# A four-layer graph network on one core: the degree sums of the first layer are added up across a block's four quarters on VectorE

## Chip, core and metric

One Trainium2 chip, one of its cores. The metric is the device time of one execution in microseconds (us); the time before is the median of three runs.

## What is computed

Four graph layers over 4096 nodes with 128 features, each on a layer-normalised, rectified copy of `x`, with a residual. Only the first layer is touched here:

```python
h = jnp.maximum(_layernorm(x, axis=-1), 0.0)
inv_deg = 1.0 / (jnp.sum(adj, axis=1) + beta)
agg = adj @ h + beta[:, None] * h
x = x + inv_deg[:, None] * agg @ kernel + bias
```

`adj` is 4096 x 4096 in float32 and mostly zero. The later layers use its nonzero entries alone, so the first layer's pass over `adj` also finds them and writes lists of them.

## The kernel before

The matrix passes through on-chip memory once, transposed by the host, in `NB` = 8 blocks of 512 destination nodes. A block is 8 MB and comes in four quarters (slots) of 2 MB; slot `q` is `ring[:, q, :, :]`, 128 partitions x 8 tiles x 512 nodes. Blocks 0 and 1 are written out, blocks 2 to 7 are one hardware loop. Each engine has its own program, and they meet at semaphores.

In block `nb`, with `last` = `nb - 1` and `before` = `nb - 2` (the lists run one to two blocks behind the loads):

- **TensorE** (`block0` of `pe`): per slot 8 products of 128x512 that add into `ps[:, 0, :]` (L1719); after the last slot four more for the `beta` term (L1726). Between the slots it makes the lists of the block before: `a_list` (L1698, 32 small products), `fold` (L1705), `places` (L1688, L1689). Then it waits for all four slots' sums, makes the degrees as products with a column of ones (L1745), waits for `agg_out` and makes `agg @ kernel` (L1753). `places` for the next block waits for `flag_ready`, which is the last thing that VectorE does in a block.
- **VectorE** (`block0` of `dve`): per slot `reduce_slot`, which adds the slot's 8 tiles down to one row of 512 sums a partition in three steps: 2048 elements (L1216), 1024 (L1217), 512 (L1221), the last into `degp[:, q, :]`. Between them the lists: `place` (L1108 to L1131), `code` (L1140, L1142, L1145; its last step releases `a_list`), `list_quarters` (L1151, waits for `a_list`), `lists` (L1163 to L1166, releases the gathers), `update` (L1232 to L1240, needs the degrees), the copy of `ps[:, 0, :]` to `aggT` (L1269, `agg_out`) and `mark` (L1100, `flag_ready`).
- **ScalarE** (`see`): for a block 128 passes over 128x128 pieces that find which hold nonzeros (L888), and the loads of the next block's slots (`load_quarter`), each when TensorE, VectorE and ScalarE have all read the slot.
- **GpSimd** gathers the listed rows of `adj` (L705, with their indices copied at L696), as the lists become ready.

A `Link` orders dependent VectorE instructions: each one counts up a semaphore, and VectorE waits for that count and passes a `nop` (`settle`) before the next one:

```python
def __call__(self, ins):
    self.n += 1
    ins.then_inc(self.s, 1)
    self.dve.wait_ge(self.s, self.base + self.n)
    settle(self.dve)
```

Of the kernel before, what the change touches and what calls it, by code (L numbers as in the profile page):

```python
# [24 lines left out]
ALU = mybir.AluOpType  # L25
# [3 lines left out]
P = 128  # L29
# [7 lines left out]
NQ = 4  # L37
# [35 lines left out]
def build(nc, x, adj_rows, k0, b0, beta, hv, w2, b2, wq, bq, wkvs, bkvs, wb, out, h1_table, h2_table, kv_table,  # L73
          adj_table, mask_table):
    ctx = ExitStack()
    with ctx:
        def sb(name, shape, dt=F32):
            return ctx.enter_context(nc.sbuf_tensor(name, shape, dt))

        def sem(name):  # L80
            return ctx.enter_context(nc.semaphore(name))
# [10 lines left out]
        ones = sb("ones", [P, P])  # L92
# [77 lines left out]
        degp = work[:, 20480:22528].rearrange("p (q n) -> p q n", q=NQ)  # L170
        half_sum = work[:, 16384:18432].rearrange("p (m n) -> p m n", m=MQ // 2)
        quarter_sum = work[:, 18432:19456].rearrange("p (m n) -> p m n", m=MQ // 4)
# [43 lines left out]
        ps = ctx.enter_context(nc.psum_tensor("ps", [P, 8, 512], F32))  # L216
# [84 lines left out]
        link_sum = sem("link_sum")  # L301
        slot_full = [sem(f"slot_full{q}") for q in range(NQ)]
        slot_used = [sem(f"slot_used{q}") for q in range(NQ)]
        slot_summed = [sem(f"slot_summed{q}") for q in range(NQ)]
# [4 lines left out]
        deg_done = sem("deg_done")  # L309
# [25 lines left out]
        def settle(eng):  # L335

            eng.nop(nofuse=True)
# [695 lines left out]
        def _(dve):  # L1033
# [178 lines left out]
            def reduce_slot(nb, q):  # L1212

                dve.wait_ge(slot_full[q], 16 * nb + 16 if not isinstance(nb, int) else 16 * (nb + 1))
                link = Link(dve, link_sum, 2, nb * NQ + q)
                link(nc.vector.tensor_tensor(half_sum, ring[:, q, 0:MQ // 2, :], ring[:, q, MQ // 2:MQ, :], ALU.add))  # L1216
                link(nc.vector.tensor_tensor(quarter_sum, half_sum[:, 0:MQ // 4, :], half_sum[:, MQ // 4:MQ // 2, :], ALU.add))  # L1217
                link.end()
                if q == 0:
                    dve.wait_ge(deg_done, nb + 1)  # L1220
                nc.vector.tensor_tensor(degp[:, q, :], quarter_sum[:, 0, :], quarter_sum[:, 1, :],  # L1221
                                        ALU.add).then_inc(slot_summed[q], 1)

# [21 lines left out]
            def block0(nb, last, before):  # L1245

                reduce_slot(nb, 0)
                if last is not None:
                    place(last)
                if before is not None:  # L1250
                    list_quarters(before, 3)
                    lists(before, 2)
                if last is not None:
                    code(last, 0)
                    update(last)
                if before is not None:
                    lists(before, 3)
                reduce_slot(nb, 1)
                if last is not None:
                    code(last, 1)  # L1260
                    list_quarters(last, 0)
                reduce_slot(nb, 2)
                if last is not None:
                    lists(last, 0)
                    code(last, 2)
                    list_quarters(last, 1)
                reduce_slot(nb, 3)
                dve.wait_ge(agg_done, nb + 1)
                nc.vector.tensor_copy(aggT[:, :], ps[:, 0, :]).then_inc(agg_out, 1)  # L1269
                if last is not None:  # L1270
                    lists(last, 1)
                    code(last, 3)
                    list_quarters(last, 2)
                mark(nb)
# [17 lines left out]
            link = Link(dve, link_s, 2)  # L1292
# [20 lines left out]
            link = Link(dve, link_s, 2, 1)  # L1313
# [131 lines left out]
            link = Link(dve, link_w, 1)  # L1445
# [3 lines left out]
            for n, rows in enumerate((wkvs_sb, bkvs_bc)):  # L1449
                ins = nc.vector.tensor_tensor_reduce(out=junks[:, n, :], in0=rows[:, 2 * P:3 * P], in1=wb_bc[:, P:2 * P], scale=1.0,  # L1450
                                                     scalar=0.0, op0=ALU.mult, op1=ALU.add,
                                                     accum_out=rows[:, 3 * P:3 * P + 1])
# [29 lines left out]
            def row_stats2(tiles):  # L1482
                for t in tiles:
                    ins = nc.vector.bn_stats(stats[:, t, :], x_sb[:, t, :])
                return ins
# [12 lines left out]
            for n in (2, 3):  # L1498
                rest2(n + 1, slice(FT * n, FT * n + FT))
                for m in range(4):  # L1500
                    t = 4 * n - 6 + m
                    products(t, t % TB)
                    ins = row_stats2(range(FT * n + 2 * m, FT * n + 2 * m + 2))
# [144 lines left out]
        def _(pe):  # L1648
            mm = nc.tensor.matmul
# [33 lines left out]
            def places(nb):  # L1683

                pe.wait_ge(flag_ready, nb + 3)
                pe.wait_ge(place_read, nb + 1)
                flags = flag[:, :, :].rearrange("p t m -> p (t m)")
                mm(ps[:, 5, 128:256], tri[:, :], flags, start=True, stop=True)  # L1688
                mm(ps[:, 5, 256:384], ones_b[:, :], flags, start=True, stop=True).then_inc(place_done, 1)  # L1689

            def a_list(nb, j):

                n = nb * TB + j
                pe.wait_ge(coded_ready, n + 1)
                pe.wait_ge(list_read, n + 1)
                for m in range(T):
                    g = m % 4
                    ins = mm(ps[NC * g:NC * g + NC, 7 if j % 2 else 3, 0:P], coded[:, j % 2, 0, :, m], onehot[:, j % 2, :, m],  # L1698
                             start=(m < 4), stop=(m >= T - 4))
                ins.then_inc(list_done, 1)  # L1700

            def fold(nb, j):

                pe.wait_ge(list_out, nb * TB + j + 1)
                mm(ps[:, 7 if j % 2 else 3, P:P + NC], quarters[:, j % 2, :], sel[:, :], start=True, stop=True).then_inc(fold_done, 1)  # L1705

            def block0(nb, last, before):
                pe.wait_ge(agg_out, 1 + nb)
                if last is not None and before is not None:
                    places(last)  # L1710
                for q in range(NQ):
                    pe.wait_ge(slot_full[q], 16 * (nb + 1))
                    for m in range(MQ):
                        t = q * MQ + m
                        if last is None and t < T // 2:
                            pe.wait_ge(ht_ready[0], t + 1)
                        elif last is None:
                            pe.wait_ge(half_relu, (t - T // 2) // TB + 1)
                        ins = mm(ps[:, 0, :], h_sb[:, q * MQ + m, :], ring[:, q, m, :],  # L1719
                                 start=(q + m == 0), stop=False)  # L1720
                    if q < NQ - 1:
                        ins.then_inc(slot_used[q], 1)
                    else:
                        pe.wait_ge(hbeta_ready, nb + 1)
                        for j in range(TB):
                            ins = mm(ps[:, 0, j * P:(j + 1) * P], hbeta[:, j, :], ident[:, :], start=False, stop=(j == TB - 1))  # L1726
                        ins.then_inc(agg_done, 1)
                    if q == 0 and last is not None and before is None:
                        places(last)
                    if q == 0 and before is not None:  # L1730
                        fold(before, 2)
                        a_list(before, 3)
                    if q == 1 and before is not None:
                        fold(before, 3)
                    if q and last is not None:
                        if q == 3:
                            fold(last, 1)
                        a_list(last, q - 1)
                        if q == 2:
                            fold(last, 0)  # L1740
                for q in range(NQ):
                    pe.wait_ge(slot_summed[q], nb + 1)
                for j in range(TB):
                    for q in range(NQ):
                        ins = mm(ps[:, 6, j:j + 1], degp[:, q, j * P:(j + 1) * P], ones[:, 0:1],  # L1745
                                 start=(q == 0), stop=(q == NQ - 1))
                ins.then_inc(deg_done, 1)
                if last is None:
                    pe.wait_ge(ld, 16 * NLD)
                pe.wait_ge(up_used, 1 + nb)  # L1750
                pe.wait_ge(agg_out, nb + 2)
                for j in range(TB):
                    ins = mm(ps[:, 1, j * P:(j + 1) * P], aggT[:, j * P:(j + 1) * P], k0_sb[:, :], start=True, stop=True)  # L1753
                ins.then_inc(up_done, 1)

            block0(0, None, None)
            block0(1, 0, None)
            with pe.Fori(2, NB) as nb:
                block0(nb, nb - 1, nb - 2)
# [191 lines left out]
```

## Time and profile before

| | |
|---|---|
| median of three runs | 1194.56 us (1192.62 to 1199.07) |
| the profiled execution | 1195.47 us, its span 1193.8 us |
| TensorE matmul busy | 895.6 us of the span (75%) |
| VectorE busy | 835.5 us (70%) |
| ScalarE busy | 681.3 us (57%) |
| GpSimd busy | 656.0 us (55%) |
| first layer with its lists | about the first 440 us of the span |

The shares are means over layers with different limits, so what the change is worth has to be read from the first 440 us alone: which engine works there without a wait, and which engines wait for it. "Granted clock" is the share of TensorE's 2.4 GHz that it was given; 1.00 is 2.4 GHz and 0.50 is 1.2 GHz. A start time plus a duration may reach past the next start, since the engine starts an instruction that it need not wait for before the one ahead has quite ended.

### The profile page before, as it was taken

The numbers are of one execution on the slowest core, as the hardware profiler recorded it, in microseconds if no ns is written. First come the engines' busy times: TensorE is split into PE (matmuls) and PEld (weight loads), VectorE is DVE, ScalarE is ACT, GpSimd is POOL, SyncE is SP. The second block draws the span as 40 slices with busy tenths as digits, with TensorE's granted clock in tenths as the row PEclk, the third lists the DMA queues.
The fourth block names the chain that finished last, engine by engine and source line by source line (L and its number), as shares of the span: only waits on it lengthen the run. The fifth ranks groups of instructions, "written<-read, shape, count | busy, mean of one in ns | idle before, by whom it ended". The sixth has DMA issues, their size and how long they took to land.

```text
span 1193.8 us, 24673 instructions
## 1 busy us (share of the span) xinstructions
PE 895.6 (75%) x5760; PEld 565.9 (47%) x5760; DVE 835.5 (70%) x2260; ACT 681.3 (57%) x3070; POOL 656.0 (55%) x662
## 2 busy tenths in 40 slices
PE   4979999999999541677667639998685888878860
PEld 1535455454554320565556525554453555555540
DVE  7378889889898774666666673121555888888888
ACT  4999887977979040344343433000364787878862
POOL 4003778764464636777777700777516666666640
PEclk9988998999989665566675569999796999999995
DMA  9656767566471217444445446993324444444421
GB/s 370 203 203 239 254 218 284 210 215 250 175 260 42 62 43 227 131 124 132 126 127 136 125 163 263 394 328 114 95 102 123 125 124 127 124 118 121 121 76 71
DMA packets 89668, 201.26 MB, mean 169 GB/s; under 512 B 20576, under 2 KB 61920, under 8 KB 83808
## 3 DMA queue, kind: packets, MB, share of 16 engines
q10 hardware_dynamic: 9216, 83.38, 18.1%
q1 hardware_dynamic: 58592, 66.35, 16.9%
q0 software_dynamic: 21760, 50.46, 15.3%
q8 instruction: 31, 0.51, 0.2%
q14 instruction: 69, 0.57, 0.1%
HBM read 168.27 MB, written 28.98 MB: 165 GB/s over the span
## 4 chain that ended last, share of the span: by engine, by line
DVE 29%; PE 26%; issue 16%; POOL 10%; DMA 8%; DVEq 3%; ACT 2%; POOLq 0%; ACTq 0%; SPq 0%
POOL work L749 9%; PE ps L1827 7%; DVE work L1216 5%; DMA work<-kv_table,node_flat 3%; DVE work L1217 3%; PE ps L1802 2%; PE ps L1871 2%; DVE work L1527 2%; DMA work<-h_table,node_flat 2%; PE ps L1880 2%; PE ps L1672 2%; DVE work L1145 2%; PE ps L1668 2%; DVE work L1140 1%; PE ps L1818 1%
## 5 line engine op out<-in xcount | busy, mean ns | idle before, releaser
L888 ACT ACTIVATE unread<-work 128x128 bf16<-128x128 f32 x1024 | 300.7, 295 | 5.1
L1719 PE MATMUL ps<-work,h_wide 128*128 128x512 f32 x512 | 242.6, 630 | 17.9 <-ACT h_wide L800 17.9
L705 POOL DMA_INDIRECT work<-in_adj_rows,adj_stage x152 | 203.9, 1342 | 66.9 <-issue 35.3
L888 ACT ACTIVATION_READ_ACCUMULATOR unread<-work 128x1 f32 x1024 | 191.1, 187 | 0.0
L749 POOL DMA_INDIRECT work<-h_table,stage x140 | 133.0, 950 | 97.3 <-DMA h_table<-h_wide 55.0
L1719 PEld LDWEIGHTS ps<-work,h_wide 128*128 128x128 f32 x512 | 102.1, 205 | 141.2 <-issue 139.4
L749 POOL DMA_INDIRECT work<-kv_table,node_flat x124 | 118.5, 955 | 89.9 <-PE ps L1890 33.4
L749 POOL DMA_INDIRECT work<-h_table,node_flat x124 | 118.0, 952 | 45.1 <-issue 37.9
L1527 DVE CUSTOM_DVE_ANT_0 work<-ps,work 128x512 f32<-128x512 f32 x168 | 116.0, 746 | 18.1 <-PE ps L1871 18.0
L981 ACT ACTIVATE work<-work 128x512 f32<-128x512 f32 x165 | 117.0, 714 | 0.9 <-DVE work L1536 0.8
L1880 PE MATMUL ps<-ident,work 128*128 128x128 f32 x648 | 93.3, 281 | 31.9 <-ACT work L981 23.0
L696 POOL COPY adj_stage<-adj_flat 128x4 int32 x38 | 20.6, 542 | 152.3 <-issue 152.1
L1698 PE MATMUL ps<-work 128*32 128x128 f16 x1024 | 68.3, 422 | 46.1 <-DVE work L1145 36.0
L1880 PEld LDWEIGHTS ps<-ident,work 128*128 128x128 f32 x648 | 71.3, 142 | 49.9 <-ACT work L981 24.2
L929 ACT ACTIVATE work<-ps 128x512 f32<-128x512 f32 x40 | 23.9, 597 | 117.9 <-PE ps L1796 115.9
L1802 PE MATMUL ps<-work 128*128 128x128 f32 x320 | 70.1, 387 | 27.7 <-ACT work L929 27.7
L1787 PE MATMUL ps<-ident,work 128*128 128x128 f32 x164 | 43.9, 421 | 61.7 <-DVE work L1353 36.3
L1827 PE MATMUL ps<-work,h_wide 128*128 128x512 f32 x192 | 85.3, 593 | 0.7 <-DVE work L1076 0.7
L1802 PEld LDWEIGHTS ps<-work 128*128 128x128 f32 x320 | 59.8, 279 | 42.3 <-ACT work L929 39.0
L1216 DVE TENSOR_TENSOR work<-work 128x2048 f32<-128x2048 f32 x32 | 73.1, 2285 | 0.0
L1142 DVE TENSOR_TENSOR work<-iota_s,slot 128x4096 f16<-128x4096 f16 x32 | 73.1, 2284 | 0.0
L1698 PEld LDWEIGHTS ps<-work 128*32 128x32 f16 x1024 | 39.0, 150 | 67.8 <-DVE work L1145 43.4
(225 smaller groups left out, 1678.1 us busy)
## 6 DMA issues: line engine op xcount, KB each, us to landing
work<-in_adj_rows ACTq DMA_DIRECT2D x38, 2048.0 KB, 7.9
work<-adj_table SPq DMA_DIRECT2D x66, 256.0 KB, 4.7
work<-in_adj_rows SPq DMA_DIRECT2D x6, 2048.0 KB, 11.8
adj_table<-work SPq DMA_DIRECT2D x80, 128.0 KB, 1.9
mask_table<-work SPq DMA_DIRECT2D x43, 128.0 KB, 1.8
work<-mask_table SPq DMA_DIRECT2D x43, 128.0 KB
kv_table<-work SPq DMA_DIRECT2D x32, 128.0 KB, 1.7
work<-work SPq DMA_DIRECT2D x43, 64.0 KB
```

The source lines that it names most:

```text
L705: nc.gpsimd.indirect_dma_start(out=ag[:, h, c, :], out_offset=None, in_=adj_rows, in_offset=bass.IndirectOffsetOnAxis(ap=adj_stage[:, h // ...
L749: nc.gpsimd.indirect_dma_start(out=rows[:, b, c, :], out_offset=None, in_=table, in_offset=bass.IndirectOffsetOnAxis(ap=at, axis=0)).then_ ...
L888: ins = nc.scalar.activation(unread[:, m % (MQ // 2) * TB + t, :], ring[:, q, m, t * P:(t + 1) * P], ACT.Abs, accum_out=seen[:, b, t, q * ...
L981: nc.scalar.activation(e[:, g.u % 2, h, :], e[:, g.u % 2, h, :], ACT.Exp, bias=nbest3[:, b, h:h + 1], scale=SCALE, accum_out=part3[:, b, h ...
L1142: nc.vector.tensor_tensor(onehot[:, b, :, :], iota_s[:, :, :], slot[:, j:j + 1, :] .to_broadcast([P, P, T]), ALU.is_equal)
L1216: link(nc.vector.tensor_tensor(half_sum, ring[:, q, 0:MQ // 2, :], ring[:, q, MQ // 2:MQ, :], ALU.add))
L1527: nc.vector.tensor_tensor_reduce(out=e[:, g.u % 2, h, :], in0=ps[:, 1 + h, :], in1=mk[:, b, :], scale=1.0, scalar=capped3[:, b, h:h + 1], ...
L1698: ins = mm(ps[NC * g:NC * g + NC, 7 if j % 2 else 3, 0:P], coded[:, j % 2, 0, :, m], onehot[:, j % 2, :, m], start=(m < 4), stop=(m >= T - 4))
L1719: ins = mm(ps[:, 0, :], h_sb[:, q * MQ + m, :], ring[:, q, m, :], start=(q + m == 0), stop=False)
L1802: ins = mm(ps[:, 4 + g.u % 2, 0:P], eT[:, c, 0, :], hg1[:, b, c, 0:P], start=(c == 0), stop=(c == QC - 1))
L1827: ins = mm(ps[:, 4 + nb, :], h_sb[:, m, :], ring2[:, q, m % MQ, :], start=(m == 0), stop=(m == T - 1))
L1880: ins = nc.tensor.transpose(ps[:, 5 + c % 2, h * P:(h + 1) * P], e[:, g.u % 2, h, c * P:(c + 1) * P], ident[:, :])
```

## The change

The four slots' sums are no longer kept apart. From the second slot on, VectorE adds the sum so far (`degp[:, q - 1, :]`) to one of its two partial rows before the last step, so that `degp[:, 3, :]` holds the sum over the whole block. TensorE then waits for the last slot's sum alone and makes four products a block with a column of ones, where it made sixteen.

```diff
             def reduce_slot(nb, q):
                 dve.wait_ge(slot_full[q], 16 * nb + 16 if not isinstance(nb, int) else 16 * (nb + 1))
-                link = Link(dve, link_sum, 2, nb * NQ + q)
+                link = Link(dve, link_sum, 3 if q else 2)
+                link.base = (3 * NQ - 1) * nb + (3 * q - 1 if q else 0)
                 link(nc.vector.tensor_tensor(half_sum, ring[:, q, 0:MQ // 2, :], ring[:, q, MQ // 2:MQ, :], ALU.add))
                 link(nc.vector.tensor_tensor(quarter_sum, half_sum[:, 0:MQ // 4, :], half_sum[:, MQ // 4:MQ // 2, :], ALU.add))
+                if q:
+                    dve.wait_ge(slot_summed[q - 1], nb + 1)
+                    settle(dve)
+                    link(nc.vector.tensor_tensor(quarter_sum[:, 0, :], quarter_sum[:, 0, :], degp[:, q - 1, :], ALU.add))
+                else:
+                    dve.wait_ge(deg_done, nb + 1)
                 link.end()
-                if q == 0:
-                    dve.wait_ge(deg_done, nb + 1)
                 nc.vector.tensor_tensor(degp[:, q, :], quarter_sum[:, 0, :], quarter_sum[:, 1, :],
                                         ALU.add).then_inc(slot_summed[q], 1)
...
-                for q in range(NQ):
-                    pe.wait_ge(slot_summed[q], nb + 1)
+                pe.wait_ge(slot_summed[NQ - 1], nb + 1)
                 for j in range(TB):
-                    for q in range(NQ):
-                        ins = mm(ps[:, 6, j:j + 1], degp[:, q, j * P:(j + 1) * P], ones[:, 0:1],
-                                 start=(q == 0), stop=(q == NQ - 1))
+                    ins = mm(ps[:, 6, j:j + 1], degp[:, NQ - 1, j * P:(j + 1) * P], ones[:, 0:1], start=True, stop=True)
                 ins.then_inc(deg_done, 1)
```

## Rows read from the trace of the kernel before

**Rows 1.** The page's busy times: us, share of the span, instructions.

```profile
PE 895.6 (75%) x5760; PEld 565.9 (47%) x5760; DVE 835.5 (70%) x2260; ACT 681.3 (57%) x3070; POOL 656.0 (55%) x662
```

**Rows 2.** Windows, one block of the loop each: length, busy time by engine, granted clock, DMA.

```profile
130.44:178.55 48.11, 45.57 (x251) 24.91 (x250) 41.96 (x77) 39.15 (x258) 38.37 (x29) 0.93 0.67 235
...
322.86:370.96 48.10, 45.09 (x251) 25.27 (x250) 41.97 (x76) 39.87 (x263) 24.79 (x20) 0.93 0.50 178
```

**Rows 3.** Waits, 226 to 322 us, two blocks: who for whom, total, times, longest.

```profile
ACT work L874 <- DVE aggT L1269: 15.7, 2, 8.0
...
PE ps L1698 <- DVE work L1145: 4.8, 2, 2.5
```

**Rows 4.** Waits of VectorE alone, 130.44 to 370.96 us, five blocks.

```profile
DVE idxf L1163 <- issue: 7.3, 12, 0.9
...
DVE work L1151 <- PE ps L1698: 0.2, 1, 0.2
```

**Rows 5.** Timeline of VectorE: start, duration, line, operation, idle time before and releaser.

```profile
230.39 0.69 DVE L1221 TENSOR_TENSOR work<-work 128x512 f32<-128x512 f32 x1
231.00 0.68 DVE L1140 TENSOR_TENSOR work<-iota_s,chunk 128x1024 f16<-128x1024 f16 x1
...
246.06 1.23 DVE L1217 TENSOR_TENSOR work<-work 128x1024 f32<-128x1024 f32 x1
247.39 0.70 DVE L1221 TENSOR_TENSOR work<-work 128x512 f32<-128x512 f32 x1
248.00 0.69 DVE L1269 COPY aggT<-ps 128x512 f32<-128x512 f32 x1
...
253.11 0.21 DVE L1100 TENSOR_SCALAR flag<-seen 128x128 bf16 x1
...
264.30 0.29 DVE L1151 COPY work<-ps 128x128 f32<-128x128 f32 x1 [0.19 <-DVE pairs L1131]
...
271.59 0.69 DVE L1240 TENSOR_TENSOR x_sb<-work,b_bc 128x512 f32 x1
272.48 0.87 DVE L1036 BATCH_NORM_STATS2 stats<-x_sb  x4 [0.19 <-DVE x_sb L1240]
```

**Rows 6.** Timeline of TensorE in the same block.

```profile
248.23 3.70 PE L1745 MATMUL ps<-ones,work 128*128 128x1 f32 x32 [0.25 <-DVE work L1221]
251.80 1.72 PE L1753 MATMUL ps<-k_sb,aggT 128*128 128x128 f32 x8
...
253.57 8.10 PE L1719 MATMUL ps<-work,h_wide 128*128 128x512 f32 x16
...
261.74 2.11 PE L1698 MATMUL ps<-work 128*32 128x128 f16 x32
```

**Rows 7.** Timeline of VectorE: ends of blocks 0, 1 and 7.

```profile
49.30 0.69 DVE L1269 COPY aggT<-ps 128x512 f32<-128x512 f32 x1 [8.13 <-PE ps L1726]
...
107.49 0.21 DVE L1100 TENSOR_SCALAR flag<-seen 128x128 bf16<-128x128 f32 x1
...
119.94 0.29 DVE L1151 COPY work<-ps 128x128 f32<-128x128 f32 x1 [1.56 <-PE ps L1698]
...
397.19 0.28 DVE L1151 COPY work<-ps 128x128 f32<-128x128 f32 x1
...
401.05 0.29 DVE L1151 COPY work<-ps 128x128 f32<-128x128 f32 x1 [3.45 <-PE ps L1698]
```

**Rows 8.** Timeline of TensorE: ends of blocks 1 and 7.

```profile
108.95 8.72 PE L1719 MATMUL ps<-work,h_wide 128*128 128x512 f32 x16
...
398.43 0.47 PE L1705 MATMUL ps<-sel,work 128*128 128x32 f32 x2
```

**Rows 9.** Timeline of GpSimd behind the last list.

```profile
438.14 0.19 POOL L696 COPY adj_stage<-adj_flat 128x4 int32 x1 [15.68 <-issue]
```

**Rows 10.** Windows of TensorE: length, busy time, granted clock, DMA share, GB/s.

```profile
252.00:256.00 4.00, 4.00 (x14) 0.57 1.01 424
...
105.50:112.50 7.00, 7.00 (x23) 0.52 1.00 426
```

## The prediction

> **What bounds the kernel now.** The page's busy row comes first [rows 1]. Over the whole span TensorE is the busiest (75%) and VectorE second (70%), so a reader might expect work moved from TensorE to VectorE to pay. That share is a mean over four layers, and the edit lies in the first alone. So next come the windows cut at the start of one and the same VectorE instruction (the first step of `reduce_slot(nb, 1)`) in consecutive blocks [rows 2]. All five blocks between 130.44 and 370.96 us take 48.1 us each. TensorE is busy 45.6 of it, VectorE 42.0, ScalarE 39. By busy time TensorE would be the bound again, with 2.5 us to spare.
>
> The waits decide. In two blocks ScalarE waits 15.7 us for VectorE's copy to `aggT`, and TensorE waits 4.8 us for VectorE's coded tile, up to 2.5 us at once [rows 3]. The other way there is next to nothing: in five blocks, 240.5 us, VectorE waits for TensorE once, 0.2 us, and for ScalarE or a load never [rows 4]. Its largest idle group is 7.3 us of "issue" in front of `lists` (L1163), which is its own sequencer reading a register and passing waits. The 6.1 us a block in which VectorE isn't busy are such gaps. So VectorE is the bound with 42.0 us busy, because each linked instruction also costs the gap behind it, and TensorE with 45.6 us busy is not. A busy PE in these views is not an engine at its limit.
>
> What hangs on VectorE's end: GpSimd sat idle 15.68 us before it copied the indices of the last lists at 438.14 us [rows 9]. From there the chain of gathers and loads starts the second layer. A microsecond added to VectorE's row of work before that point is a microsecond of the span; behind it nothing is edited.
>
> **The change, part by part.**
>
> *Added on VectorE.* Three instructions a block, 24 in all, each 128x512 in float32 from two operands: the same shape and sources as L1221, which takes 0.69 us [rows 5]. It's linked, so what counts is its pitch. From L1217's start to L1221's start are 1.33 us, of which 1.23 is the instruction: the gap of a link is 0.10 us. So 0.69 + 0.10 = 0.79 us. In front of it stand one more wait (met: the slot before is summed further up in the same row of work) and one more `nop`, whose price no row shows alone. From below it's nothing. From above: the widest gap of one link in the loop, where the count waited for is worked out in registers, is 0.20 us (271.59 + 0.69 to 272.48) [rows 5], so at most 0.20 for the second wait and 0.10 more on the first, 1.09 us together. I take 0.10 for it, as much as one link's gap, since it is the same pair of instructions: 0.89 us each, 2.67 a block, with 0.79 and 1.09 as ends.
>
> The link's gap weighs here. In front of L1140, which waits for nothing, the pitch of L1221 is 0.61 us (230.39 to 231.00) [rows 5], so a linked one costs 0.18 more. The Trainium skill, "VectorE: DVE Perf Modes", section "The DRAIN you can't avoid", says that a semaphore after each operation costs nothing extra, as the next one has to wait for the pipeline anyway. By that rule the pitch would be 0.61 and the 18 instructions in the loop would cost 11.0 us instead of 16.0; these rows speak against it.
>
> *Where it lies on the path.* Block 0: VectorE has nothing to do for 8.13 us before it copies `aggT` at 49.30 us [rows 7], so 2.67 us are hidden; without that cover they would cost all of it. Blocks 2 to 7, 18 instructions: nothing covers them, 6 x 2.67 = 16.0 us. Block 1: covered in part, since at 119.94 us VectorE waits 1.56 us for a list from TensorE [rows 7]. That list stands behind `places`, which waits for `mark`. `mark` (107.49 us) is late by 2.67, its result lands near 110.4, and TensorE's 16 products and the list after them start at about 110.6 where they start at 108.95 now [rows 8]: 1.6 us late. So 1.6 us of the 2.67 stay.
>
> *Removed on TensorE.* Twelve of sixteen products a block. All sixteen take 3.70 us [rows 6], 0.23 each, so 2.8 us go. Three waits for the slots' sums go too; they were met. In the loop, what do 2.8 us give? The degrees start when VectorE ends the fourth slot, at 248.23 us, `agg @ kernel` follows to 253.5, and the next block's products start at 253.57. But `mark` ends at 253.3 [rows 5, 6], so TensorE could start 0.2 us earlier at most: it will wait at `places` instead. The stall at L1698 and this one are TensorE's, and cost nothing. At the end of block 7 VectorE waits 3.45 us for a list, until 401.05 us [rows 7]. There the fold in front of it (L1705) starts at 398.43, after the degrees and `agg @ kernel` [rows 8], but it also needs VectorE's copy of 397.19 + 0.28 us [rows 7]. It can start at 397.6, so 0.8 us come back, not 3.
>
> *Clock.* TensorE's granted clock is 0.57 between 252 and 256 us and 0.52 between 105.5 and 112.5 us [rows 10], that is half (1.2 GHz) most of the time, right behind the degree products with their single column; each time 16 products of L1719 begin in it. They take 8.10 us and 8.72 [rows 6, 8]. In the loop the list behind them ends at 263.85 and VectorE asks for it at about 264.1 [rows 5, 6]: 0.3 us to spare. After the change TensorE idles about 2.4 us in front of these products. If the low clock then lasts as long into them as in block 1, they take 0.6 us more, and VectorE waits 0.3 a block. If it doesn't, nothing is lost. I put 0.3 in: 6 x 0.3 = 1.8 us. The two ends are nothing, and 2 us a block, if half of the products run at the low clock (8.10 / 16 = 0.5 us each, nearly twice that at half the clock: eight of them would lose some 4 us; no window here shows so long a stretch, and I take half of it as the end).
>
> *Sum* against the profiled execution: 16.0 + 1.6 - 0.8 + 1.8 = 18.6 us. The profiled execution took 1195.47 us (its span 1193.8), 0.9 above the median of 1194.56, and the sum is the same on either. From the median: 1213.2 us, 1.6% slower.
>
> **Rivals.**
>
> 1. *TensorE is the bound* and the 45.6 us rule. Then a block loses the 2.8 us of the removed products, 22 us over eight blocks: 1172 us. For it speaks the busy time alone [rows 2]; against it the 4.8 us for which TensorE waits for VectorE, while VectorE waits 0.2 us in five blocks [rows 3, 4]. It decides if VectorE's block has 2.7 us that TensorE sets, and I find none. 3%.
> 2. *Hidden.* The added work falls into waits of VectorE and the time stays, 1195 us, within the 0.5% (6 us) that this kernel's measurement can tell from no change. Only the 8.13 us of block 0, the 1.56 at block 1 and the 3.45 at block 7 are such waits [rows 7]. The loop has none. 5%.
> 3. *The list gets late.* TensorE's longer idle time keeps its clock low well into the next block's products, and VectorE waits 1 to 2 us a block for the list at L1151. This adds 4 to 10 us to the sum: 1217 to 1223 us. For it: a margin of 0.3 us only, and low clock at just this place in both windows [rows 10]. Against it: the degrees idle the array already today. The Trainium skill, "TensorE: Matmul & The Clock Gate", section "HAM oscillation — how this bites in real kernels", warns that idle gaps bring the clock down each time round; the windows agree that it falls here, and say nothing yet of longer gaps. 15%.
> 4. *The link costs less than its row*, pitch 0.61 to 0.70 us and no price for the wait: 18 x 0.65 = 11.7, with 0.8 for the two ends 12.5: 1207 us. 12%.
>
> My forecast, VectorE's row of work grows by about 2.7 us a block and nothing gives it back, has 65%, inside 1209 to 1217 us.
>
> **How the numbers follow.** The low end: 18 x 0.79 = 14.2, with 0.8 and no clock loss, 1209.6; rival 4 below it at 1207. The high end: 18 x 1.09 = 19.6 with 0.8 and 1.8 gives 1216.8; rival 3's lower part reaches 1220. So 1207 to 1220 holds about 8 in 10. Faster by over 0.5% is rival 1 (3%), within 0.5% rival 2 (5%), slower all the rest (92%).
>
> **What the profile after would show.** L1221's line shares its time with a new line of 24 instructions at 0.69 us; a block of the loop takes 50.8 to 51.1 us where it took 48.1; VectorE is busy 44.0 in it, TensorE 42.8. The degree products take about 1 us a block, and TensorE's wait moves to `places`, 2 to 2.5 us for VectorE's flag. The last lists' indices are copied by GpSimd at about 457 us instead of 438, and everything behind is unchanged in length. The step on the clock is wrong if VectorE's wait at L1151 stays at 0.2 us in five blocks, and rival 3 is right if it's over 5. I would be wrong altogether if the loop's block stayed at 48.1 us; then VectorE's gaps held slack that I took for its own work.

## The result and the profile after

The changed kernel takes 1223.75 us (median of 4 runs, 1222.71 to 1225.1) where the kernel before takes 1193.59 (4 runs, 1191.22 to 1199.07). The ratio is 1.0247, interval 1.0209 to 1.0284. So it's slower, by some 30 us and not by the 18.6 of the prediction, and the time lies above the range of 1207 to 1220. The profiled execution took 1223.54 us (span 1221.8), 28.1 more than that of before.

Start where the edit lies. These are the windows of the changed kernel, cut at the start of the same VectorE instruction (`reduce_slot(nb, 1)`), with the columns of [rows 2]:

```profile
131.95:183.25 51.30, 42.78 (x226) 22.03 (x225) 44.17 (x79) 38.99 (x258) 40.18 (x34) 0.90 0.64 227
...
336.88:388.10 51.22, 43.19 (x228) 22.28 (x227) 44.15 (x80) 39.97 (x263) 26.50 (x20) 0.90 0.47 164
sum 256.15, PE 215.28 PEld 110.68 DVE 220.37 ACT 197.84 POOL 160.29; mean PE 43.06 PEld 22.14 DVE 44.07 ACT 39.57 POOL 32.06
```

Five blocks take 256.15 us, 51.2 each, where they took 48.1: 3.1 us more (forecast 2.7 to 3.0). VectorE is 2.1 us busier in each, TensorE 2.4 less busy. What an added instruction costs is on VectorE's timeline:

```profile
236.77 1.22 DVE L1218 TENSOR_TENSOR work<-work 128x1024 f32<-128x1024 f32 x1
238.17 0.69 DVE L1222 TENSOR_TENSOR work<-work 128x512 f32<-128x512 f32 x1 [0.17 <-DVE work L1218]
238.97 0.69 DVE L1226 TENSOR_TENSOR work<-work 128x512 f32<-128x512 f32 x1
239.58 0.68 DVE L1140 TENSOR_TENSOR work<-iota_s,chunk 128x1024 f16<-128x1024 f16 x1
...
263.41 0.22 DVE L1100 TENSOR_SCALAR flag<-seen 128x128 bf16 x1
...
275.07 0.29 DVE L1151 COPY work<-ps 128x128 f32<-128x128 f32 x1 [0.66 <-PE ps L1703]
```

From L1222's start to L1226's are 0.80 us. From L1218's start to L1222's are 1.40, where the same two instructions stood 1.33 apart before [rows 5]: the second wait and `nop` cost 0.07. Together 0.87 us, forecast 0.89. The last line is VectorE's wait for the list. Over the five blocks:

```profile
DVE work L1151 <- PE ps L1703: 3.1, 5, 0.7
```

That is 0.6 a block where it was 0.2 in all five [rows 4]. 3 x 0.87 + 0.6 = 3.2, which is the 3.1 of the windows. TensorE's timeline of the same block shows why the list is late, beside [rows 6]:

```profile
258.44 1.05 PE L1748 MATMUL ps<-ones,work 128*128 128x1 f32 x8 [1.85 <-DVE work L1226]
259.36 1.14 PE L1755 MATMUL ps<-k_sb,aggT 128*128 128x128 f32 x8
263.68 0.29 PE L1693 MATMUL ps<-flag,tri 128*128 128x128 bf16 x1 [3.19 <-DVE flag L1100]
...
263.87 8.94 PE L1724 MATMUL ps<-work,h_wide 128*128 128x512 f32 x16
```

The degree products take 1.05 us for 3.70 before, and TensorE waits 3.19 us for `mark` instead (forecast 2 to 2.5). The 16 products behind take 8.94 us for 8.10. Their clock:

```profile
262.00:264.00 2.00, 0.32 (x3) 0.32 (x4) 2.00 (x5) 2.00 (x16) 1.20 (x2) 0.50 0.95 410
264.00:268.00 4.00, 4.00 (x7) 1.69 (x7) 3.72 (x4) 3.91 (x28) 3.39 (x3) 0.55 0.58 231
```

The granted clock is 0.50, then 0.55, that is nearly all at 1.2 GHz. At the end of the last block and behind it:

```profile
419.86 0.29 DVE L1151 COPY work<-ps 128x128 f32<-128x128 f32 x1 [2.65 <-PE ps L1703]
```

```profile
457.85 0.18 POOL L696 COPY adj_stage<-adj_flat 128x4 int32 x1 [16.02 <-issue]
```

The first is 3.45 us in [rows 7], so 0.8 came back, as forecast. Of that 0.6 went again right behind it: VectorE's idle times before the next two groups of `lists` are 0.86 and 0.74 us, where they were 0.46 and 0.52. The second is GpSimd's copy behind the last list, which was at 438.14 us [rows 9]: 19.7 us later, forecast 457. In the seven traces of kernels with the first layer of before (two of the kernel itself and five with waits added to TensorE's program, see the experiments) this copy comes at 437.9 to 440.5 us, in the six with the changed first layer at 457.2 to 459.2.

So the first layer is nearly as predicted. The other 8 us are lost where nothing was edited. The second layer passes the delay on: the third layer's first dense product starts at 749.06 us, 18.4 later than before. The last record of dense products starts 25.2 us later than before (853.9 us for 828.7), so the dense stretch, from the first start to the last, grew from 98.0 to 104.8 us. A further 2.9 us appear behind it, 2.1 of them in the fourth layer's scores. Their stretch is 245.6 us in this trace of the kernel before and 249.4 in another trace of the same kernel, so nothing follows from 2.1. GpSimd's timeline shows where the third layer loses its time, first the kernel before and then the changed one:

```profile
742.90 0.96 POOL L749 DMA_INDIRECT work<-h_table,stage  x1 [54.98 <-DMA h_table<-h_wide]
```

```profile
767.31 0.97 POOL L749 DMA_INDIRECT work<-h_table,stage  x1 [60.52 <-DMA h_table<-h_wide]
```

This is the first gather of the third layer's rows; it waits until all of them have been stored. It starts 12.2 us behind the first dense product in the one and 18.3 us in the other. The stores themselves, by the DMA view of the 17 us from the first dense product, first the kernel before (730.7 to 747.7 us):

```profile
q10 hardware_dynamic: 416, 6.03, 83.2%
q1 hardware_dynamic: 944, 0.95, 15.8%
q0 software_dynamic: 13, 0.04, 0.6%
...
h_table<-h_wide SPq DMA_DIRECT2D x1, 64.0 KB, 11.1
```

and the changed one (749 to 766 us):

```profile
q10 hardware_dynamic: 416, 6.03, 83.7%
q1 hardware_dynamic: 864, 0.89, 14.7%
q8 instruction: 1, 0.02, 0.3%
...
h_table<-h_wide SPq DMA_DIRECT2D x1, 64.0 KB, 17.1
```

The last number of the bottom line is the time from issue to landing: 17.1 us for 11.1. q10 carries the loads of 2 MB, the same in both. What the changed kernel has more is one packet of 16 KB on q8, a fetch of instructions, at 758.4 us, 9.4 behind the first dense product. Before, the nearest fetches on q8 lie 20.6 us ahead of that product and 32.4 behind it.

### The profile page after: what moved, and what is told of

Read it like the earlier page. It is cut to its first block, busy times and chain, and to the rows that moved or that the text cites. A ratio compares the mean times of both kernels' runs of the same rounds, so it can differ in the third digit from the quotient of the medians.

```text
span 1221.8 us, 24363 instructions
## 1 busy us (share of the span) xinstructions
PE 881.9 (72%) x5568; PEld 546.1 (45%) x5568; DVE 853.1 (70%) x2284; ACT 681.0 (56%) x3070; POOL 662.7 (54%) x662
## 4 chain that ended last, share of the span: by engine, by line
PE 29%; DVE 29%; issue 16%; POOL 8%; DMA 8%; DVEq 3%; ACT 2%; POOLq 0%; SPq 0%; ACTq 0%
POOL work L749 7%; PE ps L1829 7%; PE ps L1724 4%; DVE work L1217 4%; DVE work L1532 3%; DMA work<-kv_table,node_flat 3%; PE ps L1804 2%; DMA work<-h_table,node_flat 2%; DVE work L1218 2%; PE ps L1873 2%; DVE work L1145 2%; PE ps L1882 2%; PE ps L1677 2%; PE ps L1820 2%; DVE work L1140 2%
## 5 line engine op out<-in xcount | busy, mean ns | idle before, releaser
L1724 PE MATMUL ps<-work,h_wide 128*128 128x512 f32 x512 | 247.9, 642 | 17.0 <-ACT h_wide L800 17.0
L705 POOL DMA_INDIRECT work<-in_adj_rows,adj_stage x152 | 207.0, 1362 | 66.9 <-issue 36.3
L696 POOL COPY adj_stage<-adj_flat 128x4 int32 x38 | 23.4, 616 | 165.9 <-issue 165.8
L1804 PE MATMUL ps<-work 128*128 128x128 f32 x320 | 72.9, 399 | 27.7 <-ACT work L929 27.7
L1829 PE MATMUL ps<-work,h_wide 128*128 128x512 f32 x192 | 85.3, 593 | 0.7 <-DVE work L1076 0.7
## 6 DMA issues: line engine op xcount, KB each, us to landing
work<-in_adj_rows SPq DMA_DIRECT2D x6, 2048.0 KB, 16.1
```

The source lines that it names most:

```text
L705: nc.gpsimd.indirect_dma_start(out=ag[:, h, c, :], out_offset=None, in_=adj_rows, in_offset=bass.IndirectOffsetOnAxis(ap=adj_stage[:, h // ...
L1804: ins = mm(ps[:, 4 + g.u % 2, 0:P], eT[:, c, 0, :], hg1[:, b, c, 0:P], start=(c == 0), stop=(c == QC - 1))
L1829: ins = mm(ps[:, 4 + nb, :], h_sb[:, m, :], ring2[:, q, m % MQ, :], start=(m == 0), stop=(m == T - 1))
```

## The experiments

Every ratio is against the kernel before, run beside it on the same chip. Four groups follow.

**Both kernels again, and each half of the change alone.** e1 is the kernel before, e2 the changed one. e3 has TensorE's half only (the degrees then come from the last quarter alone, so three quarters of each sum are left out):

```
-                for q in range(NQ):
-                    pe.wait_ge(slot_summed[q], nb + 1)
+                pe.wait_ge(slot_summed[NQ - 1], nb + 1)
                 for j in range(TB):
-                    for q in range(NQ):
-                        ins = mm(ps[:, 6, j:j + 1], degp[:, q, j * P:(j + 1) * P], ones[:, 0:1],
-                                 start=(q == 0), stop=(q == NQ - 1))
+                    ins = mm(ps[:, 6, j:j + 1], degp[:, NQ - 1, j * P:(j + 1) * P], ones[:, 0:1], start=True, stop=True)
```

e4 has VectorE's half only. Its sum goes to a row that nobody reads, and TensorE keeps its 16 products:

```
+                if q:
+                    dve.wait_ge(slot_summed[q - 1], nb + 1)
+                    settle(dve)
+                    link(nc.vector.tensor_tensor(half_sum[:, 0, :], quarter_sum[:, 0, :], degp[:, q - 1, :], ALU.add))
```

Expected of e1: 

> The kernel before, unchanged, for a second trace of it. In the first traces the changed kernel is 28 us longer, of which 19.7 us lie in the first layer (up to GpSimd's copy behind the last list), and about 7 us more in the third layer, where the first gather of h2 rows starts 55 us after the layer's wait began in the one and 60.5 us in the other. Theory A (the third layer's start is a matter of chance between executions): this second trace may well show the late start too, and the time of runs of one kernel spreads by some 6 us. Theory B (it belongs to the changed kernel): this trace shows the early start again, about 742.9 us minus the little by which its first layer differs.

Of e2: 

> The changed kernel, unchanged, for a second trace. About 1223.5 us. Theory A (chance): the gathers of the third layer may start 5 us earlier against the layer's own start, with a time near 1217. Theory B (it belongs to the kernel): late again, 60 us of waiting.

Of e3: 

> TensorE's part alone: four products a block instead of sixteen, VectorE as before. The degrees then hold the last quarter's sums only. Main theory (VectorE's row of work is the bound): no more than 1 to 2 us faster, as only the end of block 7 gives 0.8 us back, and the list at L1151 may come late by up to 0.5 us a block for TensorE's lower clock (then up to 3 us slower): 1190 to 1197 us. Rival (TensorE was near enough to the bound to matter): 22 us faster, 1172. If what the third layer loses belongs to TensorE's shorter program, that part shows here: about 1200.

Of e4: 

> VectorE's part alone: the added sum with its wait and link, its result thrown away into a scratch row, sixteen products as before. Main theory: 3 x 0.87 = 2.6 us in each of six loop blocks, 15.7, and 1.6 at block 1, with the 3.45 us wait at the end of block 7 unchanged or smaller by what VectorE is late: 15 to 18 us slower in the first layer, 1209 to 1212 us. If the list comes late at L1151 because the degree products were taken away, it isn't late here: VectorE waits below 0.3 us a block there, against 0.54 to 0.68 in the changed kernel. If the third layer's loss belongs to VectorE's longer program, 1217 us.

| kernel | median us (runs) | ratio, interval | GpSimd's copy, us | first gather behind first dense product | dense stretch |
|---|---|---|---|---|---|
| e1 | 1197.67 (10) | 1.0001 [0.9985, 1.0017] | 440.05 | 12.0 | 98.7 |
| e2 | 1222.89 (4) | 1.0211 [1.0183, 1.0239] | 458.17 | 18.5 | 104.7 |
| e3 | 1203.97 (8) | 1.0051 [1.0035, 1.0068] | 439.73 | 18.3 | 105.7 |
| e4 | 1228.27 (4) | 1.0257 [1.0234, 1.0280] | 467.46 | 13.9 | 99.5 |

e2 is 24.9 us slower than the kernel before, where the first measurement had 30.2; the two intervals overlap between 1.0209 and 1.0239. Both times lie above the range.

The removed products alone change nothing in the first layer in sum (439.73 for 440.05): TensorE is not its bound. That sum hides two effects, though. From the first step of `reduce_slot(2, 1)` to that of `reduce_slot(7, 1)`, five blocks, e3 takes 244.2 us for e1's 240.7, since VectorE now waits for the list in the loop:

```profile
DVE work L1151 <- PE ps L1698: 3.0, 4, 1.7
```

(and 1.6 us more that the view puts down to "issue"). In exchange e1's wait of 3.20 us for the list at the end of block 1 is 0.20 in e3. So the list comes late in the loop with TensorE's half alone, without any added sum.

The added sums alone cost the first layer 27.4 us, where 15 to 18 were expected. TensorE's timeline of e4 says why:

```profile
262.37 5.90 PE L1750 MATMUL ps<-ones,work 128*128 128x1 f32 x32 [2.45 <-DVE work L1226]
268.13 2.05 PE L1758 MATMUL ps<-k_sb,aggT 128*128 128x128 f32 x8
```

```profile
262.00:268.00 6.00, 5.63 (x32) 5.67 (x32) 5.80 (x12) 4.13 (x24) 1.70 (x2) 0.63 0.68 241
268.00:272.00 4.00, 4.00 (x14) 2.91 (x14) 3.72 (x4) 3.91 (x28) 3.22 (x3) 0.50 0.57 231
```

TensorE waits 2.45 us for VectorE's later sum; behind that wait the granted clock is 0.63 and 0.50, and the same 16 degree products take 5.90 us for 3.70. Now TensorE is late with its list, and VectorE waits 1.4 to 3.03 us for it at the end of each block of the loop and 5.35 at the end of block 7:

```profile
281.27 0.29 DVE L1151 COPY work<-ps 128x128 f32<-128x128 f32 x1 [3.03 <-PE ps L1703]
```

So the two halves aren't additive (-0.3 and +27.4 against +18.1 together). Fewer products are worth nothing while VectorE's sum comes early, and 9.3 us once it comes late.

e3 also lost 6 us, all of it in the third layer (105.7 for 98.7 us), with a first layer like that of before. So the loss in the third layer needs neither the added sums nor a late first layer. What e3 shares with e2 is TensorE's changed half, its shorter program.

**ScalarE for a copy.** A try at giving VectorE's 0.69 us a block back: ScalarE makes the copy to `aggT`, in front of its own next work.

```
+            def copy_out(nb):
+                act.wait_ge(agg_done, nb + 1)
+                act.wait_ge(up_done, nb + 1)
+                nc.scalar.activation(aggT[:, :], ps[:, 0, :], ACT.Copy).then_inc(agg_out, 1)
...
-                nc.vector.tensor_copy(aggT[:, :], ps[:, 0, :]).then_inc(agg_out, 1)
```

Expected of e8 (on the kernel before): 

> The kernel before with the copy of the aggregate from PSUM to aggT (0.69 us, 0.61 of VectorE's row of work) moved from VectorE to ScalarE, which waits 8 us a block for it. If VectorE's row alone sets the block, 0.6 us a block are saved, 4 us in all. If TensorE's chain behind the degree products is as long (it had 0.3 us to spare at the list), at most half of it comes through and VectorE waits 0.3 to 0.5 us a block at L1151: 1 to 2 us in all.

It took 1199.35 us (10 runs), ratio 1.0025 [1.0007, 1.0044]; GpSimd's copy came at 443.17 us. No gain in sum. The five blocks of the loop did get shorter, 47.8 us for 48.1, but the first step of `reduce_slot(1, 1)` came at 86.57 us for 80.62, so more was lost in block 0 than the loop gave. What ScalarE's copy delays there stays open.

**Padding TensorE's program at its start.** Waits that are already met take place in the program and hardly any time. Put ahead of TensorE's first block they should move every later fetch:

```
+            for _ in range(153):
+                pe.wait_ge(agg_out, 1)
```

Expected of e5 (changed kernel, 153 waits): 

> The changed kernel with 153 waits, all met, put in front of TensorE's first block, where TensorE idles until 17.9 us: as many instructions as the change takes out of TensorE's program (144 loads and products and 9 waits in the three copies of a block). Theory F (the third layer is later since TensorE's shorter program moves its 16 KB instruction fetches: in the changed kernel and in the one with TensorE's part alone one fetch falls on the moment when the last h2 rows are being stored beside the slot loads, 10 us after the layer's first product, and one DMA engine's rows land 6 us late): the fetch is back 30 us earlier, GpSimd waits 55 us again instead of 60, the third layer from first to last dense product takes 98 to 99 us instead of 105, and the time is 6 to 7 us below the changed kernel's, about 1217. Theory G (it comes from the changed work itself, for example from the clock or from the order of the loads): the same 105 us and 1223.

Of e6 (kernel before, 103 waits): 

> The kernel before with 103 such waits: 256 instructions fit in a fetch, and 103 more shift the fetches as 153 fewer do. All work is that of before. Theory F: the third layer takes 105 us and GpSimd waits 60 us, so that the kernel gets 6 to 7 us slower with nothing changed, about 1204. Theory G: as before, 1198.

Of e7 (kernel before, 50 waits): 

> The kernel before with 50 such waits, between the two. Theory F: the fetch that falls at 764 us of the span comes roughly 10 to 25 us earlier, still behind the stores' end at 742 us: the third layer stays within 2 us of before's 98 us. Other fetches move too, so 1194 to 1202 us. It may show a better place, too. Theory G: as before.

e5 took 1221.95 us (4 runs), 1.0204 [1.0171, 1.0236]; e6 1195.08 (10), 0.9987 [0.9972, 1.0001]; e7 1196.76 (10), 1.0007 [0.9982, 1.0032]. The fetches moved less than I had reckoned: to 3.1 us behind the first dense product in e5, still ahead of the stores' end, and to places far from it in e6 (20.8 ahead, 32.6 behind) and e7 (48.4 ahead, 27.2 behind). The dense stretches went along: 104.2, 98.8, 99.1 us. That fits the fetch as the cause, but no kernel had changed sides. Why a pad in front of the hardware loops moves a fetch so little stays open.

**Padding behind the loops.** Before the projection to the third layer TensorE idles 21 to 23 us, and no loop lies between that point and the dense products. The waits go there:

```
             each_quad(pe, step1)

+            for _ in range(110):
+                pe.wait_ge(agg_out, 1)
             project(2)
```

Expected of e9 (changed kernel, 110 waits): 

> The changed kernel with 110 waits that are already met put into TensorE's program in the 22 us in which it stands idle before the projection to the third layer (700 to 723 us), so that nothing waits for them. Theory of the fetch (the 5 to 6 us lost in the third layer come from where a 16 KB fetch of TensorE's program falls: at 9.4 us behind the first dense product, while the last stores of h2 rows are on their way): the pad brings the fetch forward by about 180 records, to 5 to 15 us before the first dense product; GpSimd's wait for the h2 rows falls back from 60 us to 54 to 55, the third layer's dense stretch is 98 to 99.5 us for 104.7, and the time is 5 to 6 us under the changed kernel's: ratio to the kernel before 1.015 to 1.017. Rival (the loss belongs to the later start of the third layer or to the changed first layer itself, and the place of the fetch only goes along with it): wait 60 us, stretch 104 to 105 us, ratio 1.020 to 1.022.

Of e10 (kernel before, 85): 

> The kernel before with 85 met waits at the same place in TensorE's program. Theory of the fetch: the fetch that now comes 32 us behind the first dense product is brought forward by about 140 records, to 4 to 12 us behind it, onto the last stores of h2 rows; GpSimd's wait for them grows from 54.5 us to 59 to 60.5, the dense stretch from 98.7 to 104 to 106 us, and the time by 5 to 6 us: ratio 1.004 to 1.006, with the first layer untouched. Rival (the place of the fetch is no cause): wait 54 to 55 us, stretch 98 to 99.5 us, ratio 0.999 to 1.001.

Of e11 (kernel before, 200): 

> The kernel before with 200 met waits at the same place, a control for the pad itself. Theory of the fetch: the next fetch lands 10 us or more before the first dense product and the one after it 20 us or more behind, so nothing changes: wait 54 to 55 us, dense stretch 98 to 99.5 us, ratio 0.999 to 1.001. Rival (a pad of waits delays TensorE, whatever the fetch): a loss that grows with the pad, over twice that of 85 waits, ratio 1.008 or more.

In none of the three did the fetch get where I wanted it (4.4 us behind the product in e9, 27.3 in e10, 10.6 in e11). So the next three were set by these positions:

Of e12 (kernel before, 240): 

> The kernel before with 240 met waits in TensorE's idle time ahead of the projection to the third layer. With 200 of them the fetch of its program came at 10.6 us behind the first dense product and the last two of 4096 store packets of h2 rows were 2.7 us late. Theory of the fetch: 40 more waits bring it forward by about 25 records, to 4 to 8 us behind the product; the last store packets end 16.6 us behind it for 10.5, GpSimd's first gather of h2 rows comes 18 to 18.5 us behind it for 12 to 14, the dense stretch is 104 to 106 us for 98.7, and the kernel, whose first layer is that of before, takes 5 to 6 us more: ratio 1.004 to 1.006. Rival (the late stores belong to the changed kernel's later third layer, and the pad does nothing): last packet at 10.5 to 11 us, gather 12 to 15 us, ratio 1.000 to 1.002.

Of e13 (changed kernel, 240): 

> The changed kernel with 240 met waits at the same place. With 110 the fetch came at 4.4 us behind the first dense product, still ahead of the last stores, and the loss stayed. Theory of the fetch: with 240 it comes before the first dense product (by about 70 records, 3 to 8 us ahead of it), where store packets are plentiful and their queue doesn't run dry behind it; last store packet at 10.5 to 11 us, gather 12 to 14 us behind the product, dense stretch 98 to 99.5 us, 5 to 6 us gained: ratio 1.015 to 1.017. Should the fetch still fall between 0 and 10.5 us, the loss stays: 1.020 to 1.022. Rival (the place is no cause): the loss stays wherever the fetch falls.

Of e14 (changed kernel, 380): 

> The changed kernel with 380 met waits at the same place. Theory of the fetch: it comes 10 to 20 us ahead of the first dense product, the next one 15 us or more behind it, both outside the end of the stores: last store packet at 10.5 to 11 us, gather 12 to 14 us behind the product, dense stretch 98 to 99.5 us, ratio 1.015 to 1.017 (1.017 to 1.019 if so many waits outlast TensorE's idle time by a microsecond or two). Rival (the place is no cause): gather 18 us behind, stretch 104 to 105 us, ratio 1.020 or more.

All times below are us behind the third layer's first dense product. The fetches and the store packets (4096 of 512 B) were read from the DMA records of the traces; "late" is how many of the packets end more than 11.0 us behind. "Fetches" are those of q8 within 60 us. That they are TensorE's is seen from the waits: put into TensorE's program alone, they move q8's fetches, while those of the other queue with instructions, q14, stay 27 to 29 us ahead and 54 to 57 behind in the kernel before with and without waits.

```
kernel           fetches        late packets  last packet  gather  dense stretch
before           -20.6,  32.4         0          10.6       12.2       98.0
e1 before        -19.9,  32.1         0          10.6       12.0       98.7
e6 before, 103   -20.8,  32.6         0          10.9       12.6       98.8
e7 before, 50    -48.4,  27.2         0          10.5       12.0       99.1
e8 ScalarE copy  -20.4,  32.5         0          10.7       12.1       98.7
e10 before + 85  -45.1,  27.3         0          10.5       12.0       98.2
e11 before + 200 -43.0,  10.6         2          13.3       15.3      102.3
e12 before + 240 -43.7,   6.9        14          16.6       18.1      104.1
after              9.4,  55.5        14          16.6       18.3      104.8
e2 after           9.5               17          16.8       18.5      104.7
e3 TensorE half    9.4               19          16.7       18.3      105.7
e4 VectorE half  -20.0,  37.6         2          12.0       13.9       99.5
e5 after, start    3.1,  44.5        14          16.7       18.2      104.2
e9 after + 110     4.4,  52.9        14          16.7       18.1      104.0
e13 after + 240  -15.0,  42.9         3          12.5       14.4      100.8
e14 after + 380  -25.7,  27.2         0          10.5       11.9       98.7
```

| kernel | median us (runs) | ratio, interval |
|---|---|---|
| e9 | 1219.43 (6) | 1.0203 [1.0173, 1.0232] |
| e10 | 1194.97 (12) | 0.9994 [0.9976, 1.0011] |
| e11 | 1198.73 (10) | 1.0024 [1.0004, 1.0045] |
| e12 | 1204.62 (7) | 1.0058 [1.0037, 1.0080] |
| e13 | 1219.14 (5) | 1.0182 [1.0159, 1.0206] |
| e14 | 1215.95 (5) | 1.0157 [1.0135, 1.0180] |

e12 and e14 decide. e12 computes what the kernel before does in the same order; forty waits more than e11 brought the fetch onto the end of the stores, and it lost what the changed kernel loses, in the same place:

```profile
747.14 0.96 POOL L749 DMA_INDIRECT work<-h_table,stage  x1 [61.02 <-DMA h_table<-h_wide]
```

```profile
q10 hardware_dynamic: 416, 6.03, 83.7%
q1 hardware_dynamic: 883, 0.93, 15.2%
q8 instruction: 1, 0.02, 0.4%
...
h_table<-h_wide SPq DMA_DIRECT2D x1, 64.0 KB, 17.0
```

The DMA view is that of the 17 us from its first dense product at 729.01 us. e14 is the changed kernel with the fetch pushed out, and it lost nothing there, though its third layer starts as late as the changed kernel's (749.64 us):

```profile
761.58 0.97 POOL L749 DMA_INDIRECT work<-h_table,stage  x1 [54.53 <-DMA h_table<-h_wide]
```

```profile
q10 hardware_dynamic: 416, 6.03, 83.4%
q1 hardware_dynamic: 879, 0.92, 15.1%
q0 software_dynamic: 26, 0.05, 0.8%
...
h_table<-h_wide SPq DMA_DIRECT2D x1, 64.0 KB, 10.8
```

The landing takes 10.8 us and no q8 line is left in the window. The pad itself costs nothing: 85 waits leave the time as it was, and 380 waits are part of the fastest version of the changed kernel. The rival that a later third layer is what delays the stores falls with e3 and e12, which have it early and lose, and with e14, which has it late and doesn't. The rival that pads delay TensorE falls with e10 and e14.

Two things are less clean. e4 and e13 have two or three late packets (up to 1.4 and 1.9 us past the usual 10.6) with no fetch nearer than 20.0 and 15.0 us ahead, so something small besides the fetch can delay the last packets. And e11's fetch at 10.6 us, when the stores are all but done, still cost 2.7.

## Why the prediction was wrong

**The step that failed** is the last sentence of its first part, "behind it nothing is edited", with "everything behind is unchanged in length" near the end. The second layer kept its length. The third did not: its dense stretch took 104.8 us for 98.0, since the changed program of TensorE puts a fetch of 16 KB onto the end of the stores of h2 rows. Taking the products out shortened the program that stands ahead of the third layer, so its fetches fall elsewhere. No view that the prediction quotes shows instruction fetches, and the page's DMA part, which does list them, was not asked for them. No rival covered it: 1217 to 1223 us came from a late list, which wasn't what happened.

**Its sum was sound for the layer that was edited.** Point by point:

- *Bound.* Right. TensorE's half alone moved GpSimd's copy by -0.3 us (e3), so rival 1 (1172 us) and rival 2 (hidden) fall.
- *Price of an added instruction.* 0.87 us measured, 0.89 taken: 0.80 for the pitch (forecast 0.79), 0.07 for the second wait and `nop` (forecast 0.10). Over the loop 18 x 0.87 = 15.7 us. Rival 4 (0.65) falls, and with it the reading of the Trainium skill, "VectorE: DVE Perf Modes", section "The DRAIN you can't avoid", that a semaphore after each operation costs nothing extra: linked pitches are 0.80 us here, unlinked ones 0.61 (238.97 to 239.58 us above).
- *Block 0.* Right: VectorE's wait for the copy fell from 8.13 to 5.16 us, so 2.67 us and more went into it.
- *Block 1.* Mis-sized: from the first step of `reduce_slot(1, 1)` to that of `reduce_slot(2, 1)` it took 52.24 us (79.71 to 131.95) for 49.82 (80.62 to 130.44), so 2.4 us stay where 1.6 were put in. The 16 products behind `mark` took 9.19 us for 8.72, and the sum put in no lower clock for this block; VectorE's wait at L1151 fell only from 1.56 to 0.96 us.
- *Block 7.* Right at the wait (2.65 us for 3.45), but 0.6 of the 0.8 went again in front of `lists`, as shown above: 0.2 in sum.
- *Clock and late list.* The direction was right and the size half of the truth. The 16 products took 8.94 us for 8.10 (8.72 assumed), at a granted clock of 0.50 to 0.55, and VectorE waits 0.6 a block for 0.3 put in: 3.1 us in five waits, 0.2 before, so 2.9 for 1.8. e3 shows that it comes with TensorE's half. The threshold set for rival 3 was over 5 us in five blocks; 3.1 were measured. The Trainium skill, "TensorE: Matmul & The Clock Gate", section "HAM oscillation — how this bites in real kernels", names idle gaps as what brings the clock down each time round. The trace fits that, with 3.19 us idle ahead of these products, but doesn't isolate it: the clock was low there before too (0.57, behind the degree products without such a gap). In e4, with all 16 degree products behind such a gap, the first layer took 9.3 us more than in e2.
- *First layer in sum.* 15.7 + 2.4 - 0.2 + 2.9 = 20.8 by these terms. GpSimd's copy came 19.7 us later, in an execution that stood 0.9 us earlier at the first step of `reduce_slot(1, 1)`: 20.6 us of growth. e2's copy came 18.1 later than e1's, and the means of the seven and the six traces above lie 19.4 apart. Forecast 18.6.

With the fetch out of the way, as in e14, the whole change costs 1.57% [1.35, 1.80], that is 18.8 us of 1196.09 (16.1 to 21.5; the medians lie 19.9 apart), where 18.6 were forecast. That they meet so closely is luck: the terms that were too small are offset by the second layer, which gave back 1.3 us (18.4 us late at its end), and the interval is 5 us wide. The rest of the loss, about 6 us, is the fetch: e12 shows it alone at 0.58% [0.37, 0.80], 6.9 us (4.4 to 9.6; the medians lie 8.5 apart).

What stays open: 28.1 us between the two profiled executions hold 19.7 of first layer, -1.3 of second, 6.8 of third, and 2.9 behind it, which I can't tie to the change, as two traces of the kernel before differ by more there. The terms of e14 and e12 add up to 25.7 us, which is e2's 24.9 and not the 30.2 of the first measurement; the difference between those two stays open. Also open is why one packet of 16 KB holds the last 14 store packets back for 6 us. The fetch itself took 0.92 to 0.96 us. The late store packets take 27 ns each and mostly start 0.63 us apart, while a load packet of q10 takes 0.53: that looks like one DMA engine that gets through one store packet between two load packets, which is an inference, as the traces don't say on which of the 16 DMA engines a packet ran.

No version beat the kernel before. e6 (0.9987 [0.9972, 1.0001]) can't be told from it.

## What to carry to other kernels

Moving work off the busiest engine pays only if that engine is what the others wait for; ask the waits, both ways. Both halves of a swap belong in one sum: here the additions alone cost 27 us, the removed products alone gave nothing, and together they cost 18 to 20. And an edit that changes the length of an engine's program can move its instruction fetches in later stages, as it did with TensorE's here: when a stage that wasn't touched changes its length, look for the fetch queue in the DMA view of that stage, and pad the program in an idle stretch to see whether the loss moves.

## What the hardware showed that I hadn't expected

- A single fetch of 16 KB, in a stretch in which loads of 2 MB take 83% of the 16 DMA engines, delayed the last 14 to 19 of 4096 store packets by about 6 us and with them a gather and the kernel. The delay was 6.0 to 6.2 us in all six traces (five kernels) whose fetch fell 3.1 to 9.5 us behind the first dense product, 2.7 with the fetch at 10.6, and 0 to 1.9 elsewhere.
- TensorE's record of the trace holds only about one entry for two met waits put in: 85 added 43, 200 added 100.
- Sixteen products with a single column took 3.70 us behind a wait of 0.25 us and 5.90 us behind 2.45 us of waiting.
